# Conditional expert layer of an eight-stage network: shares spread over partitions, chunks interleaved

## What is computed

```python
shared_out = einsum('nh,dh->nd', silu(x_flat @ sw1.T) * (x_flat @ sw3.T), sw2)
s = sigmoid(x_flat @ router_w.T + t_bias_flat)              # n x 8
_, topk_idx = top_k(s + router_bias, 2)
s_sel = take_along_axis(s, topk_idx, axis=1)
denom = sum(s_sel, axis=1, keepdims=True)
gates = where(denom > EPS, s_sel / (denom + EPS), 1.0 / TOP_K)
combine = sum(gates[:, :, None] * one_hot(topk_idx, 8), axis=1)   # n x 8, the "shares"
H = gelu(einsum('nd,ehd->enh', x_flat, rw1))                # 8 experts of 64 hidden values
O = einsum('enh,edh->end', H, rw2)
out = (shared_out + einsum('end,ne->nd', O, combine)) / 3
```

## Time and profile before

| | us |
|---|---|
| median of 3 runs | 2887.84 |
| lowest and highest run | 2885.82, 2889.96 |
| profiled execution, its time | 2898.19 |
| profiled execution, its span | 2896.4 |
| granted TensorE clock over the span, 1.00 being 2.4 GHz | 0.828 |
| stage of the change, in the span | 973.04 to 1099.20 |

### The profile page before, as it was taken

How to read it: one execution, slowest core, us unless ns; L and a number is a source line. 1 busy time by engine, 2 the same in 40 slices (tenths; PEclk the granted TensorE clock), 3 DMA queues, 4 the chain that set the end, 5 groups by cost and what they waited for, 6 DMA issues and landing times. The chain is left out here.

```text
span 2896.4 us, 92475 instructions
## 1 busy us (share of the span) xinstructions
PE 2458.2 (85%) x37125; PEld 1765.6 (61%) x37130; DVE 1678.1 (58%) x7106; ACT 1101.8 (38%) x4210; POOL 753.1 (26%) x1226
## 2 busy tenths in 40 slices
PE   5998888884599888968999999999757878999998
PEld 3556666664355566645676766766524556777774
DVE  2543555555455454436777777776354855666674
ACT  1332333333133222324565555655354432333332
POOL 1210000000121000016677777767242310000000
PEclk9997555555599878989999999999758965999899
DMA  2000000000000000015455454545100000000000
GB/s 91 3 2 2 2 2 2 2 2 35 7 2 2 1 0 1 0 69 111 106 113 109 111 111 102 119 102 122 35 34 1 2 2 2 2 2 2 2 2 16
DMA packets 110106, 103.97 MB, mean 36 GB/s; under 512 B 90496, under 2 KB 90496, under 8 KB 108800
## 3 DMA queue, kind: packets, MB, share of 16 engines
q1 hardware_dynamic: 109696, 98.24, 13.6%
HBM read 89.81 MB, written 8.39 MB: 34 GB/s over the span
## 5 line engine op out<-in xcount | busy, mean ns | idle before, releaser
L671 POOL TENSOR_TENSOR l2r_beta_s<-l2r_state,l2r_beta_f 128x256 f32<-128x256 f32 x512 | 370.2, 744 | 191.3 <-ACT l2r_state L574 189.5
L827 DVE TENSOR_TENSOR l2r_pre<-l2r_o_ps,l2r_beta_s 128x256 f32<-128x256 f32 x512 | 197.9, 421 | 83.6 <-PE l2r_o_ps L454 74.8
L574 ACT ACTIVATE l2r_state<-l2r_pre 128x256 f32<-128x256 f32 x512 | 190.0, 417 | 50.7 <-DVE l2r_pre L827 50.0
L140 PE MATMUL l0r_bank<-main_x,l0r_wx_half 128*128 128x32 f32 (+2 forms) x480 | 150.1, 413 | 60.5 <-ACT l0r_out_gate L196 59.9
L140 PEld LDWEIGHTS l0r_bank<-main_x,l0r_wx_half 128*128 128x128 f32 x480 | 118.9, 312 | 81.6 <-ACT l0r_out_gate L196 79.5
L1824 PEld LDWEIGHTS l3r_bank<-main_x,l3r_wx_half 128*128 128x128 f32 x480 | 97.7, 230 | 93.7 <-issue 49.9
L442 PE MATMUL l2r_d_ps<-l2r_state,l2r_kq 128*32 128x128 f32 x2056 | 147.5, 279 | 0.9 <-ACT l2r_state L574 0.7
L194 ACT ACTIVATE l0r_gates<-l0r_bank 128x24 f32<-128x24 f32 x256 | 48.6, 190 | 237.0 <-PE l0r_bank L152 237.0
L1963 ACT ACTIVATE l3r_gates<-l3r_bank 128x24 f32<-128x24 f32 x256 | 48.6, 190 | 230.8 <-PE l3r_bank L1836 230.8
L1807 POOL TENSOR_SCALAR main_y<-l3r_h_ring 128x128 f32<-128x128 f32 x16 | 8.4, 528 | 479.9 <-DVE l3r_h_ring L2117 479.9
L228 DVE SCALAR_TENSOR_TENSOR l0r_both<-l0r_gates 128x16 f32<-128x16 f32 x256 | 44.6, 174 | 152.4 <-ACT l0r_gates L194 152.4
(11 more groups left out here) (585 smaller groups left out, 7149.9 us busy)
## 6 DMA issues: line engine op xcount, KB each, us to landing
l2r_beta_f<-l2r_beta_store SPq DMA_DIRECT2D x256, 256.0 KB, 3.3
main_odd_layers<-in_l SPq DMA_DIRECT2D x1, 4826.5 KB, 14.5
main_odd_layers<-in_l SPq DMA_DIRECT2D x1, 3672.0 KB, 16.3
l2r_v_store<-l2r_v_part SPq DMA_DIRECT2D x32, 96.0 KB, 5.6
l2r_v_rows<-l2r_v_store SPq DMA_DIRECT2D x16, 192.0 KB, 4.5
main_decay<-in_decay SPq DMA_DIRECT2D x1, 3072.0 KB, 9.9
main_even_layers<-in_l SPq DMA_DIRECT2D x1, 2762.5 KB, 9.6
l2r_beta_store<-l2r_beta_tok SPq DMA_DIRECT2D x128, 16.0 KB, 1.6
```

The lines of the kernel that those rows point to most:

```text
L140: nc.tensor.matmul(into, wx_half[:, g * P:(g + 1) * P], x_b[:, :, w * LW + lo:w * LW + hi].rearrange("p b t -> p t b"), start=False, stop= ...
L574: nc.scalar.activation(state[:, h * 2 * P:(h + 1) * 2 * P], pre[:, h * 2 * P:(h + 1) * 2 * P], ACT.Tanh).then_inc(state_ready[h], 1)
L671: nc.gpsimd.tensor_tensor(beta_s[:, half].rearrange("p (g r) -> p g r", g=HG), state[:, half].rearrange("p (g r) -> p g r", g=HG), beta_f[ ...
L827: nc.vector.tensor_tensor(pre[:, half].rearrange("p (c n) -> p c n", c=2), o_ps[:, 2 * h:2 * h + 2, 0:P], beta_s[:, half].rearrange("p (c ...
```

## The change

- The second layer of the routed experts no longer yields tokens on partitions. The hidden values are multiplied by the shares first (`scale_hidden`, into `scaled`), and then four products of 512 columns, each over the 128 rows of two experts, are added up in the same bank of `out_ps` as the shared expert's two (`routed_second`, `shared_second`). `acc`, its 32 multiply-adds in a chunk, the copy to it and the turn back are gone. `dst` is written from `out_ps`, whose two banks take turns between chunks.
- For that each share must stand on the 64 partitions of its expert. VectorE splits `share` into three bf16 parts (`share_parts`, 4 more instructions), TensorE turns them (`turn_shares`, 4 products of 128 columns into 24 rows), ScalarE copies them to `share_t`, and TensorE multiplies them by a matrix of zeros and ones, `pick_bf` (`spread_shares`, 4 bf16 products of 512 columns), into the banks of `h_ps` that the gelu has read.
- The loops are written out, and chunks are interleaved: `token_logits(c + 1)` comes at the end of chunk c on TensorE, `routed_second(c - 1)` after `shared_first(c)`. On VectorE `scores(c)` stands ahead of `scale_hidden(c - 1)`, and the shares' chain is cut in two around the second half of the shared expert. On ScalarE the sigmoid of the next chunk's scores comes at the end of a chunk.
- The copy to `y` is gone. GpSimd makes `pick_bf` once. The weights of layer 1 are 512 columns wider by `pick`.

```diff
+        share_parts = mem.sb("share_parts", [P, TILES, 3, NEXP], BF16)
+        share_t, pick_bf = mem.sb("share_t", [3 * NEXP, CHUNK], BF16), mem.sb("pick_bf", [3 * NEXP, CHUNK], BF16)
...
-        routed = mem.sb("routed", [P, NEXP // 2, CHUNK])
-        acc = mem.sb("acc", [P, TILES, P])
...
+        routed, scaled = mem.sb("routed", [P, PAIRS, CHUNK]), mem.sb("scaled", [P, PAIRS, CHUNK])
...
-                with pool.Fori(0, NCHUNK) as c:
-                    pool.wait_ge(s["log_psum"], c + 1)
-                    nc.gpsimd.tensor_copy(y[:, :], src[:, bass.ds(c * CHUNK, CHUNK)]).then_inc(s["y_ready"], 1)
+                nc.gpsimd.tensor_copy(pick_bf[:, :], pick).then_inc(s["pick_ready"], 1)
...
+                def token_logits(c):
+                    if c >= 1:
+                        pe.wait_ge(s["score_in"], c)
+                    for a in range(TILES):
+                        last = nc.tensor.matmul(logits[:, a, :], src[:, c * CHUNK + a * P:c * CHUNK + (a + 1) * P], router,
+                                                start=True, stop=True)
+                    last.then_inc(s["log_psum"], 1)
+
+                def shared_first(c):
+                    for n in range(2):
+                        if c >= 1:
+                            pe.wait_ge(s["scaled_ready"], PAIRS * (c - 1) + 2 * n + 2)
+                        nc.tensor.matmul(h_ps[:, 2 * n, :], sw1[:, n * P:(n + 1) * P], src[:, here(c)], start=True, stop=True)
+                        nc.tensor.matmul(h_ps[:, 2 * n + 1, :], sw3[:, n * P:(n + 1) * P], src[:, here(c)],
+                                         start=True, stop=True).then_inc(s["s_psum"], 1)
+
+                def routed_first(c):
+                    for m in range(PAIRS):
+                        pe.wait_ge(s["shared_ready"], 2 * c + m // 2 + 1)
+                        nc.tensor.matmul(h_ps[:, m, :], rw1[:, m * P:(m + 1) * P], src[:, here(c)],
+                                         start=True, stop=True).then_inc(s["r_psum"], 1)
+
+                def turn_shares(c):
+                    pe.wait_ge(s["parts_ready"], c + 1)
+                    if c >= 1:
+                        pe.wait_ge(s["share_t_ready"], c)
+                    for a in range(TILES):
+                        last = nc.tensor.matmul(turn_ps[0:3 * NEXP, a * P:(a + 1) * P],
+                                                share_parts[:, a, :, :].rearrange("p k e -> p (k e)"), ident_bf, start=True, stop=True)
+                    last.then_inc(s["turn_psum"], 1)
+
+                def shared_second(c):
+                    if c >= 2:
+                        pe.wait_ge(s["dst_ready"], c - 1)
+                    for n in range(2):
+                        last = nc.tensor.matmul(out_ps[:, c % 2, :], sw2[:, n, :], shared[:, n, :], start=(n == 0), stop=False,
+                                                skip_group_check=True)
+                    last.then_inc(s["s2_psum"], 1)
+
+                def spread_shares(c):
+                    pe.wait_ge(s["share_t_ready"], c + 1)
+                    for m in range(PAIRS):
+                        pe.wait_ge(s["gelu_ready"], PAIRS * c + m + 1)
+                        nc.tensor.matmul(h_ps[:, m, :], pick_bf[:, m * P:(m + 1) * P], share_t[:, :], start=True,
+                                         stop=True).then_inc(s["rep_psum"], 1)
+
+                def routed_second(c):
+                    for m in range(PAIRS):
+                        pe.wait_ge(s["scaled_ready"], PAIRS * c + m + 1)
+                        last = nc.tensor.matmul(out_ps[:, c % 2, :], rw2[:, m, :], scaled[:, m, :], start=False, stop=(m == PAIRS - 1),
+                                                skip_group_check=True)
+                    last.then_inc(s["out_psum"], 1)
...
-                    for e in range(NEXP):
-                        k = (NEXP + 1) * c + e + 1
-                        rows = slice(P // 2 * (e % 2), P // 2 * (e % 2 + 1))
-                        pe.wait_ge(s["routed_ready"], NEXP // 2 * c + e // 2 + 1)
-                        if e >= 1:
-                            pe.wait_ge(s["acc_ready"], TILES * (k - 1))
-                        for a in range(TILES):
-                            last = nc.tensor.matmul(out_ps[:, (e + 1) % 2, a, :], routed[rows, e // 2, a * P:(a + 1) * P],
-                                                    rw2[rows, e // 2, :], start=True, stop=True)
...
+                for c in range(NCHUNK):
+                    shared_first(c)
+                    if c >= 1:
+                        routed_second(c - 1)
+                    routed_first(c)
+                    turn_shares(c)
+                    shared_second(c)
+                    if c == 0:
+                        pe.wait_ge(s["pick_ready"], 1)
+                    spread_shares(c)
+                    if c + 1 < NCHUNK:
+                        token_logits(c + 1)
+                routed_second(NCHUNK - 1)
...
+                probabilities(0)
+                for c in range(NCHUNK):
                     for n in range(2):
                         act.wait_ge(s["s_psum"], 2 * c + n + 1)
                         nc.scalar.activation(sig[:, n, :], h_ps[:, 2 * n, :], ACT.Sigmoid).then_inc(s["sig_ready"], 1)
-                    for m in range(NEXP // 2):
-                        act.wait_ge(s["r_psum"], NEXP // 2 * c + m + 1)
-                        nc.scalar.activation(routed[:, m, :], h_ps[:, m, :], ACT.Gelu).then_inc(s["routed_ready"], 1)
+                    if c >= 1:
+                        write_out(c - 1)
+                    for m in range(PAIRS):
+                        act.wait_ge(s["r_psum"], PAIRS * c + m + 1)
+                        nc.scalar.activation(routed[:, m, :], h_ps[:, m, :], ACT.Gelu).then_inc(s["gelu_ready"], 1)
                     act.wait_ge(s["turn_psum"], c + 1)
-                    nc.scalar.activation(dst[:, bass.ds(c * CHUNK, CHUNK)], turn_ps[:, :], ACT.Identity,
-                                         scale=1.0 / 3.0).then_inc(s["dst_ready"], 1)
+                    nc.scalar.activation(share_t[:, :], turn_ps[0:3 * NEXP, :], ACT.Identity).then_inc(s["share_t_ready"], 1)
+                    if c + 1 < NCHUNK:
+                        probabilities(c + 1)
+                write_out(NCHUNK - 1)
...
+                def scores(c):
+                    dve.wait_ge(s["log_psum"], c + 1)
+                    for q in range(SEQS):
+                        half = slice(q * TILES // SEQS, (q + 1) * TILES // SEQS)
+                        last = nc.vector.tensor_tensor(score[:, half, :], logits[:, half, :],
+                                                       t_bias[:, c * SEQS + q:c * SEQS + q + 1, :].broadcast_to([P, TILES // SEQS, NEXP]),
+                                                       ALU.add)
+                    last.then_inc(s["score_in"], 1)
...
+                def route_first(c):
+                    dve.wait_ge(s["prob_ready"], c + 1)
+                    nc.vector.tensor_tensor(score, prob, over_tiles(router_bias), ALU.add).then_inc(chain, 1)
+                    largest(c, 1, picked)
+                    after(c, 6)
+                    nc.vector.scalar_tensor_tensor(score, picked, -FAR, score, ALU.mult, ALU.add).then_inc(chain, 1)
...
+                    if c >= 1:
+                        dve.wait_ge(s["turn_psum"], c)
+                    nc.vector.tensor_tensor(share_rest, share, high(share), ALU.subtract).then_inc(chain, 1)
+                    nc.vector.tensor_copy(share_parts[:, :, 0, :], high(share))
+                    after(c, 24)
+                    nc.vector.tensor_copy(share_parts[:, :, 1, :], high(share_rest)).then_inc(chain, 1)
+                    nc.vector.tensor_tensor(share_parts[:, :, 2, :], share_rest, high(share_rest), ALU.subtract).then_inc(s["parts_ready"], 1)
+
+                def shared_hidden(c, n):
+                    k = 2 * c + n
+                    dve.wait_ge(s["sig_ready"], k + 1)
+                    nc.vector.tensor_tensor(part[:, n, :], h_ps[:, 2 * n, :], sig[:, n, :], ALU.mult).then_inc(s["part_ready"], 1)
+                    dve.wait_ge(s["part_ready"], k + 1)
+                    if c >= 1:
+                        dve.wait_ge(s["s2_psum"], c)
+                    nc.vector.tensor_tensor(shared[:, n, :], h_ps[:, 2 * n + 1, :], part[:, n, :], ALU.mult).then_inc(s["shared_ready"], 1)
+
+                def scale_hidden(c):
+                    if c >= 1:
+                        dve.wait_ge(s["out_psum"], c)
+                    for m in range(PAIRS):
+                        dve.wait_ge(s["rep_psum"], PAIRS * c + m + 1)
+                        nc.vector.tensor_tensor(scaled[:, m, :], h_ps[:, m, :], routed[:, m, :], ALU.mult).then_inc(s["scaled_ready"], 1)
...
-                    dve.wait_ge(s["out_psum"], (NEXP + 1) * c + 1)
-                    nc.vector.tensor_copy(acc[:, :, :], out_ps[:, 0, :, :]).then_inc(s["acc_ready"], TILES)
-                    for e in range(NEXP):
```

(16 more changed lines are left out.)

131 lines of the change are left out of this document (53 added, 78 removed).

## The result

| | before | after |
|---|---|---|
| median, us | 2888.9 (4 runs) | 2853.8 (4 runs) |
| lowest and highest run | 2885.82, 2899.66 | 2845.99, 2859.39 |
| profiled execution: time, span | 2898.19, 2896.4 | 2852.49, 2850.4 |
| granted TensorE clock over the span | 0.828 | 0.833 |

The ratio is 0.987, with an interval of 0.984 to 0.989. A second measurement of the same two kernels gave medians of 2889.6 and 2850.2 and a ratio of 0.990 (0.986 to 0.994). Every ratio here is to executions of the kernel before that were measured beside the kernel in question, and is not the quotient of two medians: in the second measurement two of the six runs of after took 2870.9 and 2874.4 us, which moves the ratio and not the median. Medians and ratios leave out two executions (of the kernel with four repeats, experiment 6) that the chip ran in a slower state.

The account below looks back on a forecast made before the run. TensorE, at a mean granted clock of 0.69, was taken to bound the stage. 20.2 + 3 x 18.7 + 5.0 = 81.3 us instead of 126.2 gains 44.9; off the 2887.84 median that gives 2843 us, range 2832 to 2858.

Parts of the forecast that it names:

- The wait ahead of the turning: TensorE's wait in each chunk for VectorE's share chain and bf16 parts, from 13.8 to 14.5 us at the full clock.
- a later stage that gives part of the gain back: Listed sign of being wrong: a stage behind the changed one gives the gain back; later stages were forecast as long as now.
- start: From the stage's start to the end of the first spreading product: 18.6 to 20.7 us, taken as 20.2.
- chunks: Three steps between first spreading products: 17.1 us each at the full clock, 18.7 with a clock fall after the pause.
- end: After the last spreading product, one scaled, four products, latency and the write: 5.0 us, 8.4 at the half clock.
- The bf16 parts: Four new VectorE instructions splitting the shares: 0.85 us a chunk, most waiting for the one before.
- ScalarE's table load: Loading the gelu's table after writing dst: 1.28 us, costed at nothing, covered by shared_second with 0.9 us to spare.
- Rival 1: TensorE's clock stays up through the stage: stage 74.9 us, kernel 2836.5 us; chance 0.13.
- Rivals 2: Rival 2: clock low for half the stage's work, about 24 us a chunk, gain 28, kernel 2860 us; chance 0.10.
- rival 3: Clock down for the whole stage: chunk 30.2 us, stage 119.7, gain 6.5, kernel 2881 us; chance 0.03.
- rival 4: Slower: the low clock goes on into expert_stage, kernel 13.5 us slower at 2901 us; chance 0.02.
- rival 5: VectorE's queue holds TensorE more often, three 1 us handoffs more a chunk: stage 90, gain 36, kernel 2852 us; chance 0.12.

Follow-up runs that it names:

- experiment 6: After, with ScalarE repeating a 512-column activation at the stage's end: two repeats 2857.37 us, ratio 0.989; four repeats 2849.92 us, ratio 0.987.
- experiment 2: After with the chunk interleaving undone, routed second layer, write-out and scaling back in their own chunk: 2845.8 us, ratio 0.985.
- experiment 3: After with two unread products behind the next chunk's logits: 2841.17 us; separately, after with scale_hidden ahead of scores on VectorE: 2835.83 us; both ratio 0.982.
- the kernel with a quarter of the additions: Kernel before, with VectorE adding only one of four token blocks of each routed expert, TensorE's products unchanged: 2863.62 us, ratio 0.993.

## Why the prediction was right, and where it was off

**Sign and mechanism.** What was said of the stage is what the trace shows: the additions and 40 short products gone, chunks of 18.0 to 19.4 us, one pause ahead of each `shared_first` released by the second `scaled`, a low clock behind it, TensorE late at the turning. The wait ahead of the turning (0.7 us, counted for the full clock) is in chunk 0 alone, with 1.50 us. One of the prediction's own signs of being wrong came too, a later stage that gives part of the gain back; more on that below.

**The terms of the sum**, by the starts of L2211 (the forecast counts to the end of its first product, some 0.2 us later):

| term | forecast, us | measured, us |
|---|---|---|
| start | 20.2 | 17.9 |
| chunks | 3 x 18.7 = 56.1 | 18.0 + 19.4 + 18.0 = 55.4 |
| end | 5.0 | 5.6 |
| stage | 81.3 | 78.8 |

- *Start.* I took a value near the half level, because of two pauses, counted at 1.3 and 2.2 us. They were there, 0.78 and 1.50 us, each behind wide products, and the clock stayed up; experiment 2 has the same two in each chunk, also without a fall. This term is the one that missed by most, 2.3 us.
- *Chunk.* Two misses cancel. At the full clock it is 16.2 us, not 17.1: what is left of 18.0 without the 1.8 us that the slow records cost (1.79, 1.91 and 1.25 instead of 1.10, 1.02 and 1.02), and experiment 3 measured 16.30. The wait of 0.7 us ahead of the turning is not there even at the full clock: in that run the parts are ready at 1000.20 and the turning starts at 1000.37, when TensorE gets to it. The pause is 1.54 us and not 2.1, since VectorE's scores take 0.25 us and its four `scaled` 2.47, 0.62 each, where I had 0.32 and 0.72. The clock, in turn, cost 1.8, 3.2 and 1.8 us instead of 1.65: their mean of 2.3 lies nearer to the 2.6 that the rise of 5.3 us in the earlier trace rows gave.
- *The bf16 parts*, unknown and put at 0.85 us, take 0.50:

```profile
987.18 0.19 DVE L2324 TENSOR_TENSOR l1r_share_rest<-l1r_share 128x32 f32<-128x32 f32 x1
987.29 0.17 DVE L2325 COPY l1r_share_parts<-l1r_share 128x32 bf16<-128x32 bf16 x1
987.41 0.18 DVE L2327 COPY l1r_share_parts<-l1r_share_rest 128x32 bf16<-128x32 bf16 x1
987.50 0.18 DVE L2328 TENSOR_TENSOR l1r_share_parts<-l1r_share_rest 128x32 bf16<-128x32 f32 x1
```

The prediction had most of them wait for the one before. In the code only one does: L2327 needs `share_rest` and starts 0.23 us behind L2324, as a step of the chain does; the two others start 0.11 and 0.09 us behind their neighbour.

- *ScalarE's table load* is hidden, as costed. ScalarE's timeline of chunk 1:

```profile
1002.41 0.60 ACT L2247 ACTIVATE main_y<-l1r_out_ps 128x512 f32<-128x512 f32 x1 [2.84 <-PE l1r_out_ps L2217]
1003.02 1.28 ACT L2258 ACT_TABLE_LOAD   x1
1004.32 2.12 ACT L2258 ACTIVATE l1r_routed<-l1r_h_ps 128x512 f32<-128x512 f32 x4
1006.33 0.57 ACT L2260 ACTIVATE l1r_share_t<-l1r_turn_ps 24x512 bf16<-24x512 f32 x1
```

The gelu starts 0.02 us behind the load, and `share_t` is done at 1006.90, ahead of the end of `shared_second` at 1008.04. The Trainium skill (page "ScalarE: Activation LUTs", section "What ACT_TABLE_LOAD costs") adds a drain of 1380 ns to the load at each switch to another set; these rows show none, as the earlier trace rows showed none. By the Trainium skill's figure `share_t` would have been ready at 1008.28, an estimate, 0.3 us behind the start of the first spreading product; the measurement decides.

**The rivals.** Rival 1 (the clock stays up) did not come: all three pauses were followed by a fall. Experiment 3 shows what it would have been, a stage some 6.5 us shorter; I had priced it at 6.4 (81.3 - 74.9), for a kernel without the added products. Rivals 2 and 3 are excluded by the mean grant of 0.82 to 0.91 in the chunks, rival 4 by `expert_stage`, which got shorter by 1.6 to 3.3 us, rival 5 by the absence of further waits. (The parts of rival 3's chunk, with the turning at 1.2 us, add up to 30.6 us and not 30.2; nothing above rests on it.)

**From the stage to the kernel.** Here the forecast's step failed: the gain taken whole off the median, with "later stages as long as now". The stage gave 47.7 (first pair of traces) or 46.1 us (second pair), and layer 2's recurrent stage took 6.9 back in both. For the second pair the sum closes: 46.1 + 1.6 from `expert_stage` - 6.9 - 2.8 from the last recurrent stage - 3.3 from the stages ahead + 0.3 from the others = 35.0, and the spans give 2882.0 - 2847.0 = 35.0. For the first pair it is 47.7 + 3.3 - 6.9 + 0.7 + 0.9 + 0.3 = 46.0. The medians gave 35.1 and 39.4. I had allowed "as much as 4 us" for such a shift; it was more.

That the profiled execution came out at 2852.49 us, 0.8 from the 2853.3 of the forecast, is luck: 2.8 us more from the stage and 5.2 from unchanged stages stand against the 6.9 that the recurrent stage took. Nor was the whole excess of the profiled execution over the median outside the stage: in the second trace of before the stage was 2.1 us shorter. That the recurrent stage's clock falls in after is shown in two traces, why is not.

## What to carry to other kernels

When an engine's queue puts a step that waits for late data ahead of one whose data are there, move the ready one up: one exchange of two calls on VectorE was worth 11 us here, on top of a large rewrite, because the pause it removed cost its length (3 x 1.54 = 4.6 us) and more than that in clock (6.8 us). Before short products are blamed for a low clock, look for what holds TensorE between them; here it was another engine's additions. When a product leaves half of the rows of the stationary operand unused, put two of them into one: 7.36 us became 3.84 for the same sums at the same clock. And a gain measured in one stage should be checked in the stages behind it, whose clock can move although their code does not.

## What was not expected of the hardware

- A pause of 1.54 us behind the logits (8-column products) was followed by 0.50 to 0.58 of the clock in three of three chunks, and by slow records in twelve of twelve over four traces, while one of 1.50 us behind wide products was not, in any chunk of experiment 2. Whether it is the kind of product ahead of the pause that decides, no run tests. In the kernel with a quarter of the additions, 3.49 us did no harm in one chunk and 5.21 us did in the next, as shown there.
- Two products nobody reads in each of three chunks (1.54 us a chunk) made a stage 6.4 to 6.9 us shorter.
- In a recurrent stage that did not change, the granted clock fell for 20 us at the same place in two executions of one kernel, at one or two places in every other kernel with the new stage (3 to 31 us each), and, between the 35th and the 815th us of that stage, nowhere in four traces of kernels without it.
